# Context attention of the second loop: per-head products of the query-key and value-output weights, and the context of two batches prepared together

## The reference, cut to what matters

```
xn = _layer_norm(x, g1, b1)          # 256 x 128
cn = _layer_norm(context, g2, b2)    # 64 x 128
q = xn @ Wq                          # 8 heads of 64
kv = cn @ Wkv
k, v = jnp.split(kv, 2, axis=-1)
sim = jnp.einsum('bhid,bhjd->bhij', q, k) * scale      # scale = 64 ** -0.5
attn = jax.nn.softmax(sim, axis=-1)
out = jnp.einsum('bhij,bhjd->bhid', attn, v)
return out.reshape(b, n, INNER) @ Wout + bout
```

## Time and profile before

| | |
|---|---|
| runs | 2105.77, 2092.27, 2090.64 us; median 2092.27 us |
| profiled execution | 2103.81 us, span 2102.1 us, mean granted clock 0.901 |
| TensorE | busy 1798.3 us (86% of the span), 15604 matmuls |
| VectorE | 1387.6 us (66%) |
| ScalarE | 1247.6 us (59%) |
| GpSimd | 1042.5 us (50%) |
| loop_2 | 557 to 1554 us; steps 24 to 103 are ten stretches of eight steps, eight of 58.5 us, one of 60.1 us and the last of 58.2 us |

### The profile page before, as it was taken

One profiled execution on the slowest core, in us unless ns is written; L12 is line 12 of the kernel. 1 busy time (PEld: TensorE's weight loads), 2 busy tenths in 40 slices (PEclk: granted clock), 3 DMA queues, 4 the chain that ended last, 5 costly groups with the idle time before them and its releaser, 6 DMA issues. The chain is left out here.

```text
span 2102.1 us, 44035 instructions
## 1 busy us (share of the span) xinstructions
PE 1798.3 (86%) x15604; PEld 1391.5 (66%) x15604; DVE 1387.6 (66%) x4638; ACT 1247.6 (59%) x3006; POOL 1042.5 (50%) x1594
## 2 busy tenths in 40 slices
PE   3999999999588999999999999999849999569940
PEld 2666666666476778777777777877635666459940
DVE  3767777774467777777777887787646887341127
ACT  1465555654377777787777777776513777334412
POOL 0546655563335555565555565566421332246455
PEclk9789998996699999999999999999967999669975
DMA  4000000000200000000000000000000000054422
GB/s 56 9 6 14 14 15 14 8 11 8 85 1 1 5 1 7 7 7 7 7 4 4 7 7 7 4 5 5 7 24 9 22 27 19 17 117 79 66 59 81
DMA packets 70240, 44.81 MB, mean 21 GB/s; under 512 B 26560, under 2 KB 62538, under 8 KB 69834
## 3 DMA queue, kind: packets, MB, share of 16 engines
q1 hardware_dynamic: 55384, 29.79, 5.2%
q0 software_dynamic: 4608, 9.45, 3.1%
q10 hardware_dynamic: 10034, 2.77, 0.7%
HBM read 27.31 MB, written 14.16 MB: 20 GB/s over the span
## 5 line engine op out<-in xcount | busy, mean ns | idle before, releaser
L2105 POOL TENSOR_SCALAR probs<-probs,rsums 128x128 f32<-128x128 f32 (+1 forms) x512 | 208.3, 425 | 325.7 <-DVE rsums L2004 325.6
L946 POOL TENSOR_SCALAR at_least<-magnitudes,candidates 128x512 bf16<-128x512 f32 x128 | 198.0, 1563 | 210.6 <-DVE candidates L842 210.6
L1988 DVE CUSTOM_DVE_ANT_0 probs<-dist,pq,nmin 128x128 f32<-128x128 f32 (+1 forms) x512 | 181.2, 409 | 128.5 <-PE pq L1480 127.8
L1735 ACT ACTIVATE probs<-probs,low 128x130 f32<-128x130 f32 (+1 forms) x512 | 227.6, 460 | 3.7 <-DVE low L1988 3.6
L913 DVE TENSOR_REDUCE negmax<-ps_scores 128x4 f32<-128x1024 f32 x128 | 156.5, 1223 | 103.7 <-PE ps_scores L573 102.4
L731 ACT ACTIVATE pT<-ps_scoresT 128x1024 f32<-128x1024 f32 x128 | 131.2, 1025 | 77.4 <-PE ps_scoresT L582 70.4
L1998 DVE COPY pT<-pq 128x384 f32<-128x384 f32 x256 | 130.2, 550 | 2.7 <-PE pq L1495 2.7
L1657 ACT ACTIVATE qn<-pq 128x512 f32<-128x512 f32 x128 | 77.0, 602 | 79.9 <-PE pq L1352 78.4
L1480 PE MATMUL pq<-k1T,q1T 64*128 64x128 f32 (+1 forms) x1024 | 119.6, 352 | 1.5 <-DVE low L1988 1.4
L3083 POOL DMA_INDIRECT m_x<-token_rows,m_idx_put x80 | 75.8, 947 | 80.0 <-DVE m_idx_put L3013 32.8
L3035 DVE COPY m_y<-pm 128x256 f32<-128x256 f32 x40 | 17.0, 425 | 140.3 <-PE pm L2921 140.3
(11 more groups left out here) (527 smaller groups left out, 5545.4 us busy)
## 6 DMA issues: line engine op xcount, KB each, us to landing
expert_answers<-m_y SPq DMA_DIRECT2D x40, 128.0 KB, 2.1
m_w<-in_L_ffn_moe_w_dram SPq DMA_DIRECT2D x16, 256.0 KB, 6.0
x<-in_x_dram SPq DMA_DIRECT2D x16, 128.0 KB, 2.1
x_mid<-x SPq DMA_DIRECT2D x16, 128.0 KB, 1.8
y<-x_mid SPq DMA_DIRECT2D x16, 128.0 KB, 2.2
x_mid<-y SPq DMA_DIRECT2D x16, 128.0 KB, 1.8
cx<-x_mid SPq DMA_DIRECT2D x8, 256.0 KB, 3.1
token_rows<-c_hn SPq DMA_DIRECT2D x8, 256.0 KB, 2.0
```

The lines of the kernel that those rows point to most:

```text
L946: pool.tensor_scalar(at_least[:, a, :], mags[:, 512 * (a // 2):512 * (a // 2) + 512], cf[:, a:a + 1], None, ALU.is_ge).then_inc(mask_ready ...
L1735: ins = act.activation(probs[:, a, keys_nulls(i, w)], probs[:, a, keys_nulls(i, w)], ACT.Exp, bias=low[:, a, i:i + 1], scale=-1.0, accum_o ...
L1988: ins = dve.tensor_tensor_reduce(probs[:, a + t, keys(i, w)], dist[:, (1 - t) * P:N], ps[:, t * P:t * P + w], slopes[h], nmin[u][:, t, h:h ...
L2105: ins = pool.tensor_scalar(probs[:, a + t, keys(i, w)], probs[:, a + t, keys(i, w)], rsums[:, a + t, i:i + 1], 1.0, ALU.mult, ALU.mult)
```

## The change

Scores are q k^T = xn (Wq_h Wk_h^T) cn^T for each head h, and the output is attn (cn Wv_h Wo_h). The changed kernel computes the two products of weights once and uses them for all batches. Two new parts make them, in steps 2 and 4 of the first batch only: `turn_cross` transposes the three weights (12 transposes, three copies by ScalarE) and `fold_cross` multiplies them (16 matmuls of 128 columns and 64 rows, four copies). `x_q`, `x_pv` and the block-diagonal tiles are gone, with VectorE's `clear_blocks`; `kv2` is replaced by `k2` (step 16, for two batches at once, only for even u: eight matmuls of 128 columns, two banks, two copies) and `v2` (step 17, each batch: two matmuls of 512 columns, each on its own half of the array's columns, one copy). `x_scores` is one matmul of 512 columns for each half of the rows; it reads `h2T` directly. `x_out` reads the transposed probabilities directly. The context is loaded, normalised and transposed for two batches at once, in 128 rows, at the steps of the even batch.

```diff
-        c = sets(2, "cc", [S_CTX, D])
+        c = sets(2, "cc", [2 * S_CTX, D])
...
+            def turn_cross(u):
+                if u:
+                    return
+                pe.wait_ge(cross_loaded, 16 * len(cross_loads))
+                for name, src in (("wq2T", wq2[:]), ("wk2T", wkv2[:, 0:H2 * DH2]), ("wv2T", wkv2[:, H2 * DH2:])):
+                    ps = ring.open(pe, name, held=0.8)
+                    for p in range(PAIRS2):
+                        mm = pe.transpose(ps[:, p * P:(p + 1) * P], src[:, p * P:(p + 1) * P], ident[:])
+                    mm.then_inc(ring.filled(name), 1)
+
+            def fold_cross(u):
+                if u:
+                    return
+                for name in ("wk2T", "wq2T", "wv2T"):
+                    ring.wait_read(pe, name)
+                for name, left, right in (("w_qk", wk2T, wq2T), ("w_vo", wv2T, wo2[:])):
+                    for i in range(2):
+                        ps = ring.open(pe, name, i, held=0.8)
+                        rows = slice(64 * i, 64 * i + 64)
+                        for p in range(PAIRS2):
+                            mm = pe.matmul(ps[:, p * D:(p + 1) * D], left[rows, p, :], right[rows, p, :], start=True, stop=True)
+                        mm.then_inc(ring.filled(name, i), 1)
...
-            def kv2(u):
+            def k2(u):
+                if u % 2:
+                    return
...
+                ring.wait_read(pe, "cnT", u // 2)
+                for half in range(2):
+                    ps = ring.open(pe, "k2", u // 2, half, held=0.6)
+                    for j in range(4):
+                        mm = pe.matmul(ps[:, j * P:(j + 1) * P], w_qk[:, 4 * half + j, :], cnT[:], start=True, stop=True)
+                    mm.then_inc(ring.filled("k2", u // 2, half), 1)
+
+            def v2(u):
+                ps = ring.open(pe, "v2", u, held=0.6)
+                own = slice(S_CTX * (u % 2), S_CTX * (u % 2) + S_CTX)
                 for i in range(2):
-                    mm = pe.matmul(ps[64 * i:64 * i + 64, 256:512],
-                                   cnT[:], wkv2[:, H2 * DH2:].rearrange("k (p i d) -> k i p d", i=2, d=DH2)[:, i],
-                                   start=True, stop=True)
-                mm.then_inc(ring.filled("kv2", u), 1)
+                    mm = pe.matmul(ps[64 * i:64 * i + 64].rearrange("k (p d) -> k p d", d=D), cnT[:, own],
+                                   w_vo[:].rearrange("k (p i) d -> k i p d", i=2)[:, i], start=True, stop=True)
+                mm.then_inc(ring.filled("v2", u), 1)
...
-            def x_q(u):
-                ring.wait_read(pe, "h2T", u)
-                for half in range(2):
-                    ps = ring.open(pe, "q2", u, half, held=0.5)
-                    for i in range(2):
-                        p = 2 * half + i
-                        mm = pe.matmul(ps[:, i * N:(i + 1) * N], wq2[:, p * P:(p + 1) * P], h2T[:], start=True, stop=True)
-                    mm.then_inc(ring.filled("q2", u, half), 1)
-
             def x_scores(u, t):
                 if t == 0:
+                    ring.wait_read(pe, "h2T", u)
                     for half in range(2):
-                        ring.wait_read(pe, "q2", u, half)
-                    ring.wait_read(pe, "kv2", u)
+                        ring.wait_read(pe, "k2", u // 2, half)
                 ps = ring.open(pe, "s2", u, t, held=0.9)
-                for p in range(PAIRS2):
-                    mm = pe.matmul(ps[:, p * P:(p + 1) * P], q2T[:, p, t * P:(t + 1) * P], kblk[:, p, :],
-                                   start=True, stop=True)
-                mm.then_inc(ring.filled("s2", u, t), 1)
+                pe.matmul(ps[:], h2T[:, t * P:(t + 1) * P], keys2[:, u % 2].rearrange("p h k -> p (h k)"),
+                          start=True, stop=True).then_inc(ring.filled("s2", u, t), 1)
...
-            def x_pv(u):
...
-            def x_out(u):
-                for half in range(2):
-                    ring.wait_read(pe, "o2", u, half)
+                ring.wait_read(pe, "v2", u)
                 ps = ring.open(pe, "y2", u, held=0.8)
...
-                        mm = pe.matmul(ps[:, t * D:(t + 1) * D], o2T[:, p, t * P:(t + 1) * P], wo2[:, p, :],
+                        mm = pe.matmul(ps[:, t * D:(t + 1) * D], p2T[:, p, t * P:(t + 1) * P], vals2[:, p, :],
...
-                (-19, "down0"), (-18, "down1"), (22, "x_pT"), (24, "x_out"), (23, "x_pv"),
+                (-19, "down0"), (-18, "down1"), (22, "x_pT"), (24, "x_out"),
                 (-13, "k0"), (-12, "k1"), (-11, "q0"), (-10, "q1"), (-8, "null"),
-                (17, "kv2"), (17, "x_q"), (18, "xs0"), (19, "xs1"), (-5, "v0"), (1, "v1"),
+                (2, "turn_cross"), (4, "fold_cross"),
+                (16, "k2"), (17, "v2"), (18, "xs0"), (19, "xs1"), (-5, "v0"), (1, "v1"),
```

More of the change, by code:

```diff
@@ L1446, in x_pT, with x_out @@
                     mm.then_inc(ring.filled("p2T", u, half), 1)
-            def x_pv(u):
+            def x_out(u):
                 for half in range(2):
                     ring.wait_read(pe, "p2T", u, half)
[L1451 to L1455, removed]
-            def x_out(u):
-                for half in range(2):
-                    ring.wait_read(pe, "o2", u, half)
+                ring.wait_read(pe, "v2", u)
                 ps = ring.open(pe, "y2", u, held=0.8)
@@ L1552, in _ @@
                          qT0=lambda u: qk_T(u, 1, 0), qT1=lambda u: qk_T(u, 1, 1), pnT=null_probs_T,
-                         cnT=cn_T, kv2=kv2, h2T=h2_T, x_q=x_q,
-                         xs0=lambda u: x_scores(u, 0), xs1=lambda u: x_scores(u, 1), x_pT=x_pT, x_pv=x_pv, x_out=x_out,
-                         turn_null=turn_null, null_weights=null_weights)
+                         cnT=cn_T, k2=k2, v2=v2, h2T=h2_T,
+                         xs0=lambda u: x_scores(u, 0), xs1=lambda u: x_scores(u, 1), x_pT=x_pT, x_out=x_out,
+                         turn_null=turn_null, null_weights=null_weights, turn_cross=turn_cross, fold_cross=fold_cross)
             order = [
@@ L1680, in null_probs_T, with turn_cross, fold_cross @@
                 act.activation(pnT[:], ps[0:32, 0:N], ACT.Copy).then_inc(ring.read("pnT", u), 1)
+            def turn_cross(u):
+                if u:
+                    return
+                for name, dst in (("wq2T", wq2T), ("wk2T", wk2T), ("wv2T", wv2T)):
+                    ps = ring.wait(act, name)
+                    act.activation(dst, ps[:].rearrange("p (c n) -> p c n", n=P), ACT.Copy).then_inc(ring.read(name), 1)
+            def fold_cross(u):
+                if u:
+                    return
+                for name, dst, scale in (("w_qk", w_qk, DH2 ** -0.5), ("w_vo", w_vo, 1.0)):
+                    for i in range(2):
+                        ps = ring.wait(act, name, i)
+                        act.activation(dst[:].rearrange("k (p i) d -> k i p d", i=2)[:, i],
+                                       ps[:].rearrange("k (p d) -> k p d", d=D), ACT.Copy, scale=scale)\
+                            .then_inc(ring.read(name, i), 1)
@@ L1682, in cn_T @@
             def cn_T(u):
+                if u % 2:
+                    return
                 if u == 0:
                     act.wait_ge(cross_loaded, 16 * len(cross_loads))
[L1685 to L1692, removed]
-                    act.activation(kblk[rows, :, 64 * i:64 * i + 64],
-                                   ps[rows, 0:256].rearrange("d (p k) -> d p k", p=PAIRS2), ACT.Copy)
-                    ins = act.activation(vblk[rows, :, 64 * i:64 * i + 64],
-                                         ps[rows, 256:512].rearrange("k (p d) -> k p d", p=PAIRS2), ACT.Copy)
-                ins.then_inc(ring.read("kv2", u), 1)
+                ps = ring.wait(act, "cnT", u // 2)
@@ new lines, in cn_T, with k2 @@
+                affine(cnT[:], ps[:, 0:2 * S_CTX], ln_c).then_inc(ring.read("cnT", u // 2), 1)
+            def k2(u):
+                if u % 2:
+                    return
+                for half in range(2):
+                    ps = ring.wait(act, "k2", u // 2, half)
+                    act.activation(keys2[:, :, 4 * half:4 * half + 4, :].rearrange("p b h k -> p h b k"),
+                                   ps[:].rearrange("p (h b k) -> p h b k", b=2, k=S_CTX), ACT.Copy)\
+                        .then_inc(ring.read("k2", u // 2, half), 1)
@@ L1699, in h2_T, with v2 @@
+            def v2(u):
+                ps = ring.wait(act, "v2", u)
+                act.activation(vals2[:].rearrange("k p d -> k (p d)"), ps[:], ACT.Copy).then_inc(ring.read("v2", u), 1)
             def h2_T(u):
@@ L1701, in h2_T @@
                 affine(h2T[:], ps[:, 0:N], ln_x).then_inc(ring.read("h2T", u), 1)
-            def x_q(u):
-                for half in range(2):
-                    ps = ring.wait(act, "q2", u, half)
-                    act.activation(q2T[:, 2 * half:2 * half + 2, :].rearrange("p c n -> p (c n)"), ps[:], ACT.Copy,
```

(10 more changed lines are left out.)

76 lines of the change are left out of this document (41 added, 35 removed), and 2 rows, old and new, of the table order.

## The result

The changed kernel takes 2078.28 us (median of 15 runs, 2069.32 to 2098.61); the kernel before took 2091.80 beside it (15 runs, 2082.62 to 2105.77). The ratio is 0.9918, with a 95% interval of 0.9892 to 0.9944. The prediction was 2081 us, in a range of 2053 to 2099. The profiled execution took 2077.49 us, with a span of 2075.7.

The account below looks back on a forecast made before the run. TensorE bounds the kernel on average, but VectorE sets the pace up to x_out. From the median 2092.3 us, -35.4 + 14.1 - 4.5 - 1.6 - 2 - 1.2 + 6 + 13 = -11.6 gives 2081 us, range 2053 to 2099.

Parts of the forecast that it names:

- kv2 and x_q out, v2 in: Step 17, 16 batches, TensorE: 3.16 us removed, v2 adds 0.95; gain 2.21 a batch, 35.4 us in all.
- k2: Step 16, 8 times, TensorE: 16 records add 1.76 us each time, 14.1 us in all, with nothing to hide it.
- x_pv swallowed: Step 23: removed 1.73 us turns into x_out's wait, 1.55 to 3.28 us, ten times; only 4.5 us gained, in the tail.
- Rival C: At x_out: x_pv's 1.73 us are gained, the stall stays 1.55 us; -42 us, 2050 us; chance 0.14.
- The clock: After x_out's ten longer stalls: eight more half-clock stretches of 1.6 us each, 13 us lost (0 to 16).
- Rival B: At x_out: the stall grows but the clock holds, so no 13 us loss; -24.6 us, 2068 us; chance 0.18.
- E: At x_out: low clock after 3.28 us stalls lasts twice as long; +5 us, 2097 us; chance 0.07.
- Tail: End of loop 2: last scores no longer wait for query copies, 1.2 us; x_pv's 4.5 us also falls there.
- scores and context: Steps 18, 19: wider score matmuls gain 0.1 us a batch, 1.6 us; context in pairs gains TensorE 2 us (0 to 4).
- Products: Steps 2 and 4, once: weights' transposes and products take TensorE 4.8 us, with some waits 6 us (3 to 10).
- Rival D: In the scores: few wide matmuls cost less than their columns, 14 us more gained, 2067 us; chance 0.09.

Follow-up runs that it names:

- a6: Changed kernel with x_out's result y2 kept off the banks that the current step's scores and transposes hold: 2050.3 us, ratio 0.9777 to the kernel before.
- c1: a6 with k2 also issued one step earlier: 2060.4 us, ratio 0.9842 to the kernel before.
- a1: Changed kernel with unused TensorE work of x_pv's size put back in step 7, where x_pv was: 2077.8 us, ratio 0.9932 to the kernel before.
- a8: Changed kernel with unused TensorE work of x_pv's size put into step 1, where x_q stood: 2155.1 us, ratio 1.0100 to the kernel before.
- b1: Query-key half of the change alone, with context in pairs and x_pv kept: 2065.5 us, ratio 0.9858 to the kernel before.
- b2: Value-output half of the change alone, put into the kernel before, x_pv gone: 2118.7 us, ratio 1.0125 to the kernel before.
- r1: The changed kernel again, unaltered, for one more profile: 2123.1 us (one run), loop 2 998.1 us.
- r0: The kernel before again, unaltered, for one more profile: 2134.4 us (one run), loop 2 1011.7 us.
- c2: a6 with ScalarE's activations of up0 issued ahead of the copy that waits for TensorE: 2101.3 us, ratio 0.9846 to the kernel before.
- a2: Changed kernel with x_out issued one step earlier, in step 7, its bank planned as held longer: 2053.8 us, ratio 0.9800 to the kernel before.
- a4: Changed kernel with one Newton step instead of three in VectorE's query and key norms: 2044.7 us, ratio 0.9751 to the kernel before.
- a5: Changed kernel with k2 one step earlier on TensorE and ScalarE: 2067.5 us, ratio 0.9868 to the kernel before.

## Why the prediction was right

Its mechanism held step by step: x_pv's time went into a longer wait for VectorE, and half clock followed nearly every one of these waits. No step failed; some sizes were off, and part of the closeness is luck: the sizes that were too large and too small partly cancel, and the two pairs of profiles give -6.3 and -13.6 us for loop 2 where -11.6 was predicted.

- **kv2 and x_q out, v2 in: -2.21 a batch.** Step 57 went from 7.87 to 5.73 us, -2.14. v2 took 1.00 us, not 0.95.
- **k2: +1.76, eight times.** In a6, with a steady clock, step 64, which has k2, is 1.6 us longer than step 56 without it (10.8 and 9.2). In c1 the step that k2 moved into is 1.79 us longer.
- **x_pv swallowed.** The wait was predicted at 3.28 us and is 3.2 to 3.3, ten times. a1, a8, b1 and b2 show the cause. That steps 103 to 127 gain nothing by it held as well: step 103 is 1.54 us shorter and step 104 1.54 us longer. Rival C is out for this change: its time is what a6 reaches, by the other bank that C named.
- **The clock, 13 us for eight more stretches.** There are seven more (nine against two; r1 against r0: six more). Without them steps 24 to 103 should take 586.4 less 3.2 (two stretches today), less 21.4 (step 1), plus 8.8 (five k2), 570.6 us: the measured 584.8 leave 14.2, 1.6 us for each of the nine. The changed kernel shows the price directly too: of its batches with a k2 the one without half clock (from step 32) took 57.66 us, three with one stretch of 3.4 us 59.30 to 59.38. Against a6 it is 11 us for nine, 1.2 each. Rival B, at 0.18, is out. So is E: two of the nine stretches lasted twice as long, the others did not.
- **Tail.** From step 104 to loop 2's end 188.2 became 178.9 us (190.6 and 179.0 in the second pair), -9 to -12. The terms that fall there (x_pv 4.5, copies 1.2, five batches' 2.2, scores and context 1, less two k2) make -14.2: 3 to 5 us less came than was counted. The shortfall lies behind step 126, where these terms make -8.3 and 58.0 became 53.9 us (59.0 and 54.1). The last x_pv gave 3.1 us between transposes and bias matmul (3.6 in the second pair), not 4.0, and the last x_out took 3.78 us instead of 2.05, in both pairs: half clock, which I had not counted there. It was granted for 26.6 us of this end, where it had been for 13.6 (23.4 and 16.5). The tail is the term that was most mis-sized.
- **Products, 6 us.** Steps 2 and 4, which hold them, grew by 1.7 and 2.9 us, 4.6 in all. Steps 0 to 23 together went from 155.4 to 158.8 us, +3.4, where the same terms (6, k2 1.8, less 2.2 and less x_pv's 1.7) make +3.9. That these are so close is chance: step 8 also grew by 1.3 us, for a longer stretch of half clock, and it was as long in r0 without the change (9.39 us before, 10.71 changed, 10.75 in r0).
- **Rival D** is out. The scores of half the rows took eight records of 128 columns and 1.00 us to the next start; now they take two of 512 columns, as many columns in all, and 0.96 us. D wanted less than half of that. The wide records save next to nothing.

Together loop 2 shrank by 6.3 us in the first pair and by 13.6 in the second, 10 on average, against -11.6 predicted. The medians differ by 13.5 and the ratio gives 17 (12 to 23). What lies between these and loop 2's 10 us stays open; with unchanged loops that vary by 10 us from one execution to the next, two pairs of profiles can't tell it. For the same reason c2's ratio (0.9846) and a6's (0.9777) stand 0.7% apart with equal loops 2, on two chips.

What the prediction did not draw from its own reading: it knew that y2's bank was the trouble, and the change as predicted gave 14 us, while with the bank of a6 it gives 41. How much that bank alone would give in the kernel before was not tried.

## What to carry to other kernels

Before taking work off the busiest engine, find for each piece the next wait behind it and who ends that wait: work ahead of a wait for another engine is free to keep and worth nothing to remove, and removing it can cost clock. The same 1.7 us a batch cost 27.6 us in one step and nothing in another; half of this change beat the whole. When a wait goes, look which engine ends the next one before moving more work there, and where a planner picks banks, see whether it hands a late-read bank to an operation that need not wait, and which operation gets that bank next.

## What the runs showed of the hardware

**How often low clock follows a wait.** The granted clock falls from full to one half (1.2 GHz of 2.4). After a wait of 1.0 to 1.1 us: none of 25 (a6, c2, and five batches of c1). After 1.31: 4 of 10 (a2). After 1.4 to 1.6: 2, 3, 3, 2 and 2 of 10 (before, r0, a1, b1, a4) and none of 5 (a5). After 2.05: 5 of 5 (c1). After 3.28: 9 and 9 (changed, r1), 8 (a8) and 6 (b2) of 10, and 4 of 5 (a5). So the length of the wait goes with it but does not decide it alone. In the changed kernel the fall came between 1.4 us before the end of the wait and 1.6 us after it. In b2 TensorE has 3.6 us of work in step 1 where the changed kernel has 1.0; whether that is why its clock held more often was not tried.

**The unchanged first loop has two ends.** It took 553.7 us in the profile of before and 557.9 in b1, and 541.3 to 550.5 in the twelve others. The windows from 485 to 545 us, near its end, before and then changed:

```profile
485.00:545.00 60.00, 54.12 (x388) 35.90 (x386) 19.12 (x67) 19.50 (x28) 21.08 (x29) 0.56 0.03 8
```

```profile
485.00:545.00 60.00, 41.66 (x415) 28.53 (x412) 21.66 (x80) 19.32 (x29) 27.00 (x38) 0.76 0.04 11
```

The loop's code is the same, and the granted clock of these 60 us is 0.56 in one and 0.76 in the other, with 388 matmul records done against 415. What brings the one or the other stays open. The total of a single profile is no measure of 1%; a loop cut out of it is a better one (loop 2 differed by 7.5 us, 0.7%, between before and r0, and by 0.1 between changed and r1).

**One wait of 25 us without a releaser.** The four profiles a8, c2, r0 and r1, all from one chip, have it once in the mixture of experts of phase 3 (25.0 to 28.5 us), none of the other ten. In r0:

```profile
2052.65 3.75 PE L2921 MATMUL pm<-m_w,m_hid 128*128 128x128 f32 x16 [24.97 <-issue]
```

It would be most of the 40 us by which that chip's runs are longer. What it is stays open.
